# One stage for the Q, K, V projections and self-attention of a decoder layer on one NeuronCore: new order of batches and of the first two heads

## The reference, cut to what matters

```python
# B, N, D, H = 4, 1024, 256, 16; DK = 16
def _msa(x, w_qkv, w_proj):
    qkv = (x @ w_qkv).reshape(b, n, 3, H, DK)
    q, k, v = (qkv[:, :, i].transpose(0, 2, 1, 3) for i in range(3))
    attn = jnp.einsum('bhnd,bhmd->bhnm', q, k) * (1.0 / np.sqrt(DK))
    attn = jax.nn.softmax(attn, axis=-1)
    y = jnp.einsum('bhnm,bhmd->bhnd', attn, v)
    ...
x = x + _msa(_layernorm(x, ln1_w, ln1_b), w_qkv, w_proj)
```

## Time and profile before

| | |
|---|---|
| median of 3 runs | 1658.89 us (1657.52 to 1659.37) |
| the profiled execution | 1659.65 us |
| its span, first to last instruction | 1657.7 us |
| PE busy | 1521.3 us (92%) |
| DVE busy | 1118.0 us (67%) |
| ACT busy | 885.4 us (53%) |
| POOL busy | 402.5 us (24%) |
| mean granted clock of PE | 0.964 of full speed |

### The profile page before, as it was taken

The page is one execution under the profiler, slowest core; times in us unless marked ns, Lnnn a source line. Parts: engine busy times, 40 slices in busy tenths (PEclk is TensorE's granted clock), DMA queues, the critical chain, the costliest instruction groups (busy, mean ns, idle before and its releaser), DMA issues. The chain is left out here.

```text
span 1657.7 us, 46015 instructions
## 1 busy us (share of the span) xinstructions
PE 1521.3 (92%) x18412; PEld 1080.4 (65%) x18413; DVE 1118.0 (67%) x1679; ACT 885.4 (53%) x1589; POOL 402.5 (24%) x718
## 2 busy tenths in 40 slices
PE   6999699977886999999999999999999669999997
PEld 3555466654542676666666766676658658889886
DVE  4547398886636888898889888988846633323232
ACT  1222466554441888888888888888884211222211
POOL 3110223213331111111111111111111025555553
PEclk9999799999996999999999999999999779999999
DMA  7000000001222111111111111111106645555562
GB/s 225 0 2 17 20 1 2 1 2 39 114 114 77 33 41 40 38 37 41 40 38 37 41 40 38 37 41 39 38 8 203 215 165 194 176 195 187 176 203 64
DMA packets 80311, 125.11 MB, mean 75 GB/s; under 512 B 22243, under 2 KB 46437, under 8 KB 80134
## 3 DMA queue, kind: packets, MB, share of 16 engines
q1 hardware_dynamic: 74518, 107.24, 21.3%
q0 software_dynamic: 5616, 15.34, 2.7%
HBM read 96.03 MB, written 26.08 MB: 74 GB/s over the span
## 5 line engine op out<-in xcount | busy, mean ns | idle before, releaser
L1287 DVE TENSOR_REDUCE sb_m_mx<-banks 128x1 f32<-128x1024 f32 x512 | 603.2, 1219 | 70.5 <-PE banks L1155 62.8
L1253 ACT ACTIVATE sb_m_pT<-banks 128x512 f32<-128x512 f32 x1024 | 556.6, 595 | 117.5 <-PE banks L1182 106.3
L1182 PE MATMUL banks<-sb_m_q,sb_m_k 99*32 99x512 bf16 x4096 | 467.1, 381 | 0.8 <-ACT sb_m_pT L1253 0.5
L1155 PE MATMUL banks<-sb_m_k,sb_m_q 96*32 96x512 bf16 x4096 | 367.8, 388 | 12.9 <-DMA sb_m_k<-k_parts 10.5
L1197 PE MATMUL banks<-sb_m_pT,sb_m_v 128*32 128x256 f32 x4096 | 314.4, 378 | 0.7 <-ACT sb_m_pT L1253 0.7
L1182 PEld LDWEIGHTS banks<-sb_m_q,sb_m_k 99*32 99x32 bf16 x4096 | 178.8, 96 | 78.8 <-ACT sb_m_pT L1253 6.0
L1155 PEld LDWEIGHTS banks<-sb_m_k,sb_m_q 96*32 96x32 bf16 x4096 | 160.4, 97 | 93.0 <-DVE sb_m_mx L1287 19.3
L1197 PEld LDWEIGHTS banks<-sb_m_pT,sb_m_v 128*32 128x32 f32 x4096 | 177.5, 109 | 58.1 <-ACT sb_m_pT L1253 1.2
L1819 ACT ACTIVATE sb_e_hT<-banks 128x512 f32<-128x512 f32 x78 | 46.6, 597 | 240.0 <-PE banks L1778 240.0
L1125 POOL CAST sb_m_mx_parts<-sb_m_mxT 8x128 bf16<-8x128 f32 x64 | 18.1, 283 | 592.2 <-issue 564.2
L1789 PE MATMUL banks<-w,sb_e_hT 128*128 x624 | 143.9, 384 | 9.7 <-ACT sb_e_hT L1819 6.4
(11 more groups left out here) (219 smaller groups left out, 1916.5 us busy)
## 6 DMA issues: line engine op xcount, KB each, us to landing
w<-in_w SPq DMA_DIRECT2D x47, 1024.0 KB, 5.3
sb_m_q<-q_parts SPq DMA_DIRECT2D x384, 32.0 KB, 1.8
sb_m_k<-k_parts SPq DMA_DIRECT2D x384, 32.0 KB, 1.8
q_parts<-sb_c_parts SPq DMA_DIRECT2D x24, 256.0 KB, 2.2
k_parts<-sb_c_parts SPq DMA_DIRECT2D x24, 256.0 KB, 2.3
X<-in_x SPq DMA_DIRECT2D x4, 1024.0 KB, 10.7
x_rows<-X SPq DMA_DIRECT2D x8, 512.0 KB, 9.2
z_rows<-sb_g_zs SPq DMA_DIRECT2D x8, 512.0 KB, 4.8
```

The lines of the kernel that those rows point to most:

```text
L1155: mm = pe.matmul(ps[2 * (k % 2) + h][c:c + 32, :], q_s[0:R, i, k * P + c:k * P + c + 32], k_s[0:R, i, h * 512:(h + 1) * 512], start=True, ...
L1182: mm = pe.matmul(ps[rotating(use)][c:c + 32, :], k_s[:, i2, m * P + c:m * P + c + 32], q_s[:, i2, h * 512:(h + 1) * 512], start=True, stop ...
L1253: act.activation(pT[:, m, h * 512:(h + 1) * 512], ps[rotating(f"b{m}{h}")][:, :], ACT.Exp).then_inc(exped, 1)
L1287: dve.tensor_reduce(mx[:, par % 2, k:k + 1], pz[:, 2 * (k % 2):2 * (k % 2) + 2, :].rearrange("p q n -> p (q n)"), AX.X, ALU.max).then_inc( ...
```

## The change

The two stages become one function, `project_and_attend`. With the letters of above:

- **Start.** The clearing of `k_s` on DVE and of `v_s` on POOL now stands at the head of the joint stage, and PE waits for it there.
- **Batches 0 to 2.** The loops are written out. PE turns the tiles of batch b+1 *before* the values of batch b, into the other of two `xT` buffers; ACT takes the first half of them before *middle* of unit 3 of batch b and the second half after it. `xs` and one `xT` lie in the second half of `y_all`, the other `xT` and the rests in memory of earlier stages.
- **Batch 3** has no place of its own: its eight half units stand between A(0) to A(7) of head 0 on PE (slot 0), its eight values between A(0) to A(7) of head 1 (slot 1). On DVE *rest* of unit 0, 1, 2, 3 stands behind the maxima of A(0), A(2), A(4), A(6) of slot 0.
- **SP** loads head 0 after the stores of batch 1, head 1 after those of batch 2, head 2 after those of batch 3.
- **The barrier** between the stages is gone.

From slot 2 on the order within attention is as it was. The diff, cut to its core:

```diff
+def project_and_attend(nc, ctx, t, dram):
...
+        @block.sync
+        def _(sp):
...
+            for b in range(B):
+                for u in range(U):
+                    store(b, u)
+                if b == 1:
+                    batch_stored(0)
+                    load(0, 0)
+                if b == 2:
+                    load(1, 1)
+
+            def slot(s, par, it, edge):
+                if s > 0 and has(s, -1, edge):
...
+                    load(s + 1, (par + 1) % NB)
+                if has(s, 1, edge):
+                    i, _ = turn(par, it, 1)
+                    sp.wait_ge(split_done, s)
+                    for r in range(3):
...
+        @block.tensor
+        def _(pe):
+            pe.wait_ge(set_up, 3)
+            pe.wait_ge(w_in, 48)
+
+            def turn_tiles(b):
+                pe.wait_ge(xs_done, b + 1)
...
+            def unit(b, u, h):
+
+                if u == 0:
+                    pe.wait_ge(xT_copied, 4 * b + 2 * h + 2)
+                if h == 0 and u < 2:
+                    need(pe, v_copied, v_ready(b - 1) - 1 + u if b else 0)
+                elif h == 0:
+                    pe.wait_ge(rest_done, U * b + u - 1)
...
+            def values(b, i):
+
+                last = b == B - 1
+                if i % 4 == 0:
+                    pe.wait_ge(rest_done, U * b + U - 1 + i // 4)
...
+            turn_tiles(0)
+            for b in range(B - 1):
+                for u in range(U):
+                    unit(b, u, 0)
+                    unit(b, u, 1)
+                turn_tiles(b + 1)
+                for i in range(TPB):
+                    values(b, i)
...
+                if s == 0:
+                    unit(B - 1, 0, 0)
+                    for k in range(TPB):
+                        if k < TPB - 1:
+                            unit(B - 1, (k + 1) // 2, (k + 1) % 2)
+                        a(k)
+                    return
+                if s == 1:
+                    for k in range(TPB):
+                        values(B - 1, k)
+                        a(k)
+                        if k == 2:
+                            maxima()
+                    return
...
+        @block.scalar
+        def _(act):
...
+            for b in range(B):
+                for u in range(U):
+                    if u >= 1:
+                        middle(b, u - 1)
+                    high(b, u)
+                if b < B - 1:
+                    take_tiles(b + 1, 0)
+                middle(b, U - 1)
+                if b < B - 1:
+                    take_tiles(b + 1, 1)
+                    for u in range(2):
+                        act.wait_ge(v_done, 2 * b + u + 1)
+                        take_values(b, 4 + 2 * u, 4 * u, 2)
...
+        @block.vector
+        def _(dve):
+            dve.memset(k_s[R:R + 3, :, :], -1.0).then_inc(set_up, 1)
+            dve.sem_inc(xs_done, 1)
...
+                for k in range(4):
+                    top(k)
+                    if s == 0 and k in (0, 2):
+                        remainder(B - 1, k // 2)
...
+                for k in range(4, TPB):
+                    top(k)
+                    if s == 0 and k in (4, 6):
+                        remainder(B - 1, k // 2)
...
                 with ExitStack() as ahead:
-                    tensors(ahead, [("w_qkv", [P, KT, 3 * D], F32), ("ln1_w", [P, KT], F32), ("ln1_b", [P, KT], F32),
-                                    ("xs_c", [P, TPB, D], F32)])
+                    tensors(ahead, [("w_qkv", [P, KT, 3 * D], F32), ("ln1_w", [P, KT], F32), ("ln1_b", [P, KT], F32)])
...
                     run(cross_attention)
-                    run(project_qkv)
-                run(self_attention)
+                    run(project_and_attend)
```

More of the change, by code:

```diff
@@ L1908, in decoder @@
                 with ExitStack() as ahead:
-                    tensors(ahead, [("w_qkv", [P, KT, 3 * D], F32), ("ln1_w", [P, KT], F32), ("ln1_b", [P, KT], F32),
-                                    ("xs_c", [P, TPB, D], F32)])
+                    tensors(ahead, [("w_qkv", [P, KT, 3 * D], F32), ("ln1_w", [P, KT], F32), ("ln1_b", [P, KT], F32)])
+                    half = t["y_all"][:, B * H // 2:, :, :].rearrange("p h n d -> p (h n d)")
+                    t["xs_c"] = half[:, 0:TPB * D].rearrange("p (n d) -> p n d", d=D)
+                    t["xT_mem"] = half[:, TPB * D:].rearrange("p (k n) -> p k n", k=KT)
                     t["qkv_in"] = ahead.enter_context(nc.semaphore("qkv_in"))
                     run(cross_attention)
-                    run(project_qkv)
-                run(self_attention)
+                    run(project_and_attend)
             tensors(attention, [("w2", [P, E, HT, D], F32), ("logits", [P, NT, E], F32), ("token_from", [P, J], U32),
```

358 lines of the change are left out of this document (added).

## The result

| | before | changed |
|---|---|---|
| median | 1658.38 us (4 runs, 1657.52 to 1659.37) | 1648.99 us (4 runs, 1645.81 to 1650.76) |
| profiled execution | 1659.65 us, span 1657.7 | 1650.76 us, span 1648.7 |

The ratio is 0.9941, with a 95% interval of 0.9923 to 0.9959: 9.4 us less, faster by more than the 0.2% that can be told. Forecast were 1650.1 us and a gain of 8.8. Five further runs of the changed kernel beside the last experiments gave 1648.6 us and 0.9947 (0.9934 to 0.9961).

A forecast was written before the change was run, and what follows sets the result against it. PE bounds the long stretch after self-attention's start, which the change leaves alone; in the 144 us before slot 2, +3.3 + 6.7 - 18.8 = -8.8 us gives 1650.1 us against the median 1658.89, range 1641 to 1657.

The forecast's parts named there:

- the finish line: First score tile of slot 2 on PE, at 533.80 us before; the stretch up to it was forecast 8.8 us shorter.
- the start: Start of the stage: the clearing of `k_s` on DVE, hidden before, delays the end of batch 0's second norm by 3.3 us.
- the hand-overs: Three waits from a batch's second norm's end to the next batch's units: 11.1 us each, 33.3 instead of 26.6, +6.7 us.
- the way behind T of batch 3: From the start of batch 3's units to slot 2's first real score tile: 34.4 us instead of 53.2, -18.8 us.
- N - T: Per batch, start of its units on PE to end of its second norm on DVE: 19.9 us, taken as unchanged.
- slow burst of transposes: PE's first transposes in the stage: at a slow clock they would be absorbed, since DVE's chain is late by as much.
- The first rival: PE's clock holds after each batch's second norm: 8.9 us to the next units, 6.6 less in all, 1643.5 us; chance 0.24.
- a pair of half unit and A(k): Slot 0 on PE: half a unit and one score tile by turns, 2.25 us a pair, with DVE keeping up.
- the hole of 2.5 us that I put at T + 19: PE idle some 2.5 us, 19 us after batch 3's units start, waiting for the maxima of slot 0.
- SP's queue: Head 0's maxima, issued behind head 2's load until 32.9 us after batch 3's units start, hold slot 2; 3 us lost.
- rival of a half clock in slots 0 and 1: Two rivals: half clock in slot 1 only, 1656.2 us, chance 0.13; in slots 0 and 1 both, 1671.7 us, chance 0.07.
- removed register instructions: Removed loops and register instructions, counted as unissued rest and costed at nothing, as standing in no chain.

The follow-up runs named there:

- the hole filled: Changed kernel plus six extra matmuls with unread results on PE, between unit 3 and the next batch's transposes; 1645.9 us (one run).
- the old order of the hand-over: Changed kernel with both groups of values put back ahead of the next batch's transposes on PE, and ACT's order put back; 1638.62 us.
- without interleaving: Changed kernel with batch 3 given a place of its own again, slots 0 and 1 holding only score tiles; 1653.71 us (one run).

## Why the prediction was right

**The time.** 1648.99 against 1650.1 us, a gain of 9.4 against 8.8. The stretch up to the finish line, the only one that the sum speaks of, gained 8.9 us against 8.8. That close a fit is luck, for the errors cancel: measured less forecast is +0.5 us at the start, -0.3 in the hand-overs, +0.6 on the way behind T of batch 3, and -0.8 in N - T, which I had held fixed. The four runs of the changed kernel lie 5 us apart.

**The start.** +3.3 forecast, +3.8 in the profile; taking it away gave 4.5 at N of batch 0 and 3.5 at the finish. I had DVE start 0.3 us earlier than its statistics did; its clearing started 0.45 us later (2.45 us behind the last matmul, where the statistics had 2.0). The slow burst of transposes (3.68 us, half clock) was absorbed but for some 0.3 us: without it the statistics came 4.2 us earlier and N 4.5.

**The hand-overs.** +6.7 forecast, +6.4 measured (33.0 against 26.6). Both halves of the reason hold when taken apart: 8.8 us of queue (8.9 forecast) with the hole filled, and 2.1 and 2.3 of clock (2.2 forecast). The rule cited from the Trainium skill, TensorE: Matmul & The Clock Gate, section "HAM oscillation — how this bites in real kernels", agrees with all three hand-overs of the changed kernel, each at a granted clock of 0.50, and its cure with the first two hand-overs of the filled hole, at 1.00; the third, with 2.38 us of idle time left, fell to 0.56. The first rival, that the clock holds, fell.

**The way behind T of batch 3.** -18.8 forecast, -18.2 measured. The split into 11.2 (joint stage) and 7.0 (interleaving) was not in the prediction. The terms inside it were mis-sized: a pair of half unit and A(k) takes 2.46 us (496.60 to 499.06), not 2.25, and a pair of value and A(k) 1.61, not 1.35 to 1.4. Either pair is about 0.2 us longer than its parts in unbroken rows (1.75 + 0.5 and 0.9 + 0.5); why, was not tried. So PE, not DVE, sets most of slots 0 and 1: the hole of 2.5 us that I put at T + 19 is one of 0.49 us, and PE is through at T + 33.2 instead of T + 31.4 to 32. The total hardly shows it, because SP's queue ended last, and that chain was forecast well: stores issued by T + 25.3, load of head 2 by 30.8, maxima by 32.9, and 26.0, 31.7 and 33.9 in the profile. It costs 1.8 us instead of nearly 3. Neither rival of a half clock in slots 0 and 1 came: interleaved with units and values the score tiles ran at full clock (1.00 in both rows above), alone they did not.

**What I left out.** I had written that the forecast is wrong if anything from slot 2 on differs, and this sign came. Slot 2 now starts at full clock, 1.00 in its row, where before it ran at 0.83 of full speed up to 548:

```profile
533.80:548.00 14.20, 14.20 (x222) 6.55 (x215) 11.47 (x11) 10.43 (x20) 1.64 (x5) 0.83 0.09 20
```

It takes 12.3 us up to the turned maxima instead of 14.2. The prediction took it over unchanged. N - T, also taken over, fell by 0.4 us: 0.3 of it lie between the end of *low* and the *high* that waits for its store (3.55 us instead of 3.84). The removed register instructions, costed at nothing, may be the cause; that was not tried.

## What to carry to other kernels

Moving a step earlier helps only if its input is there earlier, and what it is moved past may have been filling a hole: here the transposes waited for the same norm as before, and the values lost their place. Put between the two, so that one group fills the hole and the transposes run the moment their input is there, the same buffer gave 5.3 us instead of 11.0. A hole into which work is moved must still be there when the other edits are in, so its owner has to be read again from the profile of the combination.

## What the runs showed of the hardware that was not expected

- A TensorE idle for 5.7 us had fallen to 1.2 GHz in all six hand-overs of two executions of the changed kernel, and the transposes behind ran at it. After 1.3 and 1.8 us of idle time with a group of values between, as in the old order in the new stage, it stayed at 2.4 GHz in all three. The kernel before, with waits of 1.6 to 1.7 and then 2.1 us in each hand-over, had fallen in the first two and not in the third: the same order of work gives either. So does slot 2: behind the same wait of 1.24 us for the maxima it began at 1.00 in the changed kernel, and at 0.60 with the old order of the hand-over, where it took 13.5 us up to the turned maxima instead of 12.3:

```profile
515.24:519.50 4.26, 4.26 (x46) 1.74 (x50) 1.74 (x3) 2.92 (x6) 0.82 (x3) 0.60 0.33 77
```

- Score tiles on 32 columns each, four side by side, did not hold the full clock where DVE paced them: 0.62 on average over the 19 us of slots 0 and 1 without interleaving, with PE busy for 15.0 of them.
